# A decoder kernel's selective scan: the carried state is copied by GpSimd at its own wait instead of by VectorE, under new instruction orders

## The reference

```
x = layernorm(x + L0_attn(x))            # selective scan (below)
x = layernorm(x + L0_xattn(x, ctx))      # similarity, norm, softmax
x = layernorm(x + L0_ffn(x))             # 8 experts of width 176, top 2, and a shared one of 352
x = layernorm(x + L1_attn(x))            # gated linear recurrence
x = layernorm(x + L1_xattn(ctx, x))      # top-76 mask of a 256x256 similarity, per batch
x = layernorm(x + L1_ffn(x))             # 8 experts of width 128, top 2, and a shared one of 256
```

```
hidden = silu(conv(W_in x) + bias)            dts = softplus(W_dt dt + b_dt)
dA[n]  = exp(dts * A[:, n])                   dBu[n] = dts * B[n] * hidden
state[n] = dA[n] * state[n] + dBu[n]          (along the 256 positions)
y = sum over n of C[n] * state[n] + D * hidden
```

## Time and profile before

| | |
|---|---|
| median of 3 runs | 695.41 us |
| the profiled execution | 695.28 us, span 693.5 us |
| VectorE busy | 574.6 us (83% of the span) |
| TensorE busy | 553.7 us (80%) |
| ScalarE busy | 440.4 us (64%) |
| GpSimd busy | 228.8 us (33%) |
| mean granted TensorE clock | 0.873 |
| chain that ended last | PE 37%, DVE 35%, issue 14%, ACT 11% |

### The profile page before, as it was taken

The page is one execution under the profiler, slowest core; times in us unless marked ns, Lnnn a source line. Parts: engine busy times, 40 slices in busy tenths (PEclk is TensorE's granted clock), DMA queues, the critical chain, the costliest instruction groups (busy, mean ns, idle before and its releaser), DMA issues.

```text
span 693.5 us, 8972 instructions
## 1 busy us (share of the span) xinstructions
PE 553.7 (80%) x2504; PEld 395.2 (57%) x2504; DVE 574.6 (83%) x1307; ACT 440.4 (64%) x959; POOL 228.8 (33%) x280
## 2 busy tenths in 40 slices
PE   5753454988799875999899799888499999979957
PEld 3532242666567653667656575656366766657634
DVE  1179999999899979999999998999998999672442
ACT  3688354878689364889784879397167988232211
POOL 1055555423223345434332452343023435010000
PEclk9976575898799975899999989999589999989968
DMA  6580100570053400660162010461054037006000
GB/s 211 165 351 0 60 1 1 143 255 1 1 149 104 132 8 1 169 229 1 54 194 64 28 63 1 115 222 54 1 170 152 2 113 209 1 12 207 2 8 8
DMA packets 29297, 63.56 MB, mean 92 GB/s; under 512 B 4864, under 2 KB 8192, under 8 KB 28736
## 3 DMA queue, kind: packets, MB, share of 16 engines
q1 hardware_dynamic: 29248, 62.98, 29.4%
HBM read 61.85 MB, written 1.11 MB: 91 GB/s over the span
## 4 chain that ended last, share of the span: by engine, by line
PE 37%; DVE 35%; issue 14%; ACT 11%; DMA 1%; DVEq 1%; POOL 0%; SPq 0%; POOLq 0%; ACTq 0%
PE work L545 24%; DVE st L1077 8%; DVE acc L1093 6%; PE h_bank L521 4%; PE work L596 4%; ACT dA L877 3%; PE work L521 3%; DVE carry L1101 3%; DVE h_tok L1001 3%; DVE m L1042 2%; DVE wk L1046 2%; DVE row L937 2%; DVE bst L929 2%; ACT L877 1%; ACT xsT L757 1%
## 5 line engine op out<-in xcount | busy, mean ns | idle before, releaser
L496 POOL TENSOR_TENSOR dbu<-du,b_rows 128x512 f32<-128x512 f32 x128 | 165.2, 1292 | 139.5 <-DVE st L1077 112.7
L877 ACT ACTIVATE dA<-dts,a_neg 128x128 f32<-128x128 f32 x512 | 160.1, 390 | 31.2 <-DVE st L1077 30.6
L1077 DVE TENSOR_TENSOR_SCAN st<-dA,dbu 128x516 f32<-128x516 f32 x128 | 165.4, 1295 | 3.2 <-issue 2.0
L521 PE MATMUL h_bank<-ident,st 128*128 128x128 f32 x512 | 93.9, 315 | 59.3 <-DVE st L1077 59.0
L521 PEld LDWEIGHTS h_bank<-ident,st 128*128 128x128 f32 x512 | 70.3, 162 | 95.4 <-DVE st L1077 76.9
L545 PE MATMUL work<-stream,xsT 128*128 128x352 f32 x320 | 116.0, 504 | 0.5 <-ACT h_tok L757 0.3
L1093 DVE SCALAR_TENSOR_TENSOR acc<-h_bank,c_cols,acc 128x512 f32<-128x512 f32 x128 | 93.2, 728 | 12.2 <-PE h_bank L521 11.7
L545 PEld LDWEIGHTS work<-stream,xsT 128*128 128x128 f32 x320 | 63.0, 211 | 28.8 <-issue 7.9
L757 ACT ACT_TABLE_LOAD x46 | 59.0, 1283 | 7.4 <-PE work L545 6.7
L877 ACT ACT_TABLE_LOAD x46 | 59.0, 1283 | 0.8
L1001 DVE SCALAR_TENSOR_TENSOR h_tok<-h_tok,wf,work 128x128 f32<-128x128 f32 (+2 forms) x136 | 43.6, 372 | 18.9 <-PE work L545 18.7
(11 more groups left out here) (154 smaller groups left out, 860.7 us busy)
## 6 DMA issues: line engine op xcount, KB each, us to landing
stream<-in_stream SPq DMA_DIRECT2D x80, 352.0 KB, 3.6
stream<-in_stream SPq DMA_DIRECT2D x32, 384.0 KB, 3.8
b_rows<-b_dram SPq DMA_DIRECT2D x32, 256.0 KB, 5.4
stream<-in_stream SPq DMA_DIRECT2D x8, 256.0 KB, 3.3
wg<-in_wg SPq DMA_DIRECT2D x1, 1280.0 KB, 8.2
wu<-in_wu SPq DMA_DIRECT2D x1, 1280.0 KB, 10.8
wd<-in_wd SPq DMA_DIRECT2D x1, 1280.0 KB, 13.3
xT<-in_xT SPq DMA_DIRECT2D x4, 256.0 KB, 4.0
```

Of the source, the lines that this page charges most:

```text
L496: gp.tensor_tensor(tile[:, :, 1:1 + w * P], du[:, batch % 2, :, lo:hi], b_rows[:, b % 2, k:k + 1, :].to_broadcast([P, ET, P]), ALU.mult).t ...
L521: return nc.tensor.transpose(dst, src, ident[:, :])
L877: last = A(dA[:, i % DA_RING, t, 1:1 + w * P], dts[:, batch % 2, t, lo:hi], ACT.Exp, scale=a_neg[:, t, k:k + 1])
L1077: V.tensor_tensor_scan(st[:, i % ST_RING].rearrange("p t l -> p (t l)"), dA[:, i % DA_RING].rearrange("p t l -> p (t l)"), dbu[:, i % DBU_ ...
```

## The change

GpSimd's loop gets the copy: ahead of dbu number i, behind the wait for scan number i - 3 that it makes anyway, it copies the last column of that scan into `carry` (if that scan belongs to an even group). VectorE's copy and its two waits are taken out. The four strings of `ORDER` and `BANK` are replaced.

```diff
 ORDER = {
     "pe": [
-        "pp000apppssppaaaaaaaaaaaaaspssppsssssssssssssss0s00sss00000sssss0000s0s00s00s000s0000s000sss00000s000101s00spp",
+        "ppa0aaaaaaaaaaaaa00pppssppsspssppssssssssssssss0s00sss00000sssss0000ss000s00s000s000s0s00ss000000s000saaspps01",
...
     "dve": [
-        "saa00111pppppppppsssssssapsssssssssassa00sss0s00ss0s0s0s00as00s0s00s000sa000000ss0000000assaasa0aa00000sas0s00",
-        "pppp010saaaa1a0100a100a11p0s0000011s1s11s000000ss111s000000011111aasasa0a000aas1s11111ssa00sss0aaas00s0s0s0s00",
+        "saa00111ppppaaaaapppppsssssssasspsssssssaassa00assas0s00ss0s0s0s00s00s0s00s000s000s000s0000000ssass0aaas00000s",
+        "pppp0a00a1sss1s0101s11011p100s11s00ss011100000s11111ss000000ssaaas0000000aass0s000001s1111sa0a001aa0s0s0s00s00",
...
     "act": [
-        "p0p00appspaaaaaaaaaaapssspsssppssspssssssssssss000ssss00sss000ss0s0000s00s000000ss0000000ss0000sss000aaa1000s1",
+        "pa0paaaaaaaaaaa00ppsppssspssspspssspsssssssssss000ssaaass00sss000ss0s0000ss00000ss0000000000ss0000ssss000asp00",
...
@@ -486,6 +486,12 @@
                     if i >= DBU_RING:
                         pool.wait_ge(s["scan_done"], i - DBU_RING + 1)
+                    g, n = divmod(i - DBU_RING, N)
+                    if g >= 0 and hands_on(g):
+
+                        if hands.index(g):
+                            pool.wait_ge(s["carried"], (hands.index(g) - 1) * N + n + 1)
+                        gp.tensor_copy(carry[:, n, :], st[:, (i - DBU_RING) % ST_RING, :, P]).then_inc(s["carry_ready"], 1)
                     tile = dbu[:, i % DBU_RING]
@@ -1094,12 +1100,6 @@
                                 .then_inc(s["acc_done"], 1)
-                        if hands_on(b):
-                            dve.wait_ge(s["scan_done"], b * N + n + 1)
-                            if hands.index(b):
-                                dve.wait_ge(s["carried"], (hands.index(b) - 1) * N + n + 1)
-                            V.tensor_copy(carry[:, n, :], st[:, (b * N + n) % ST_RING, :, w * P])\
-                                .then_inc(s["carry_ready"], 1)
                 if stage == "out" and k == 2:
```

More of the change, by code:

```diff
@@ L88 @@
     "pe": [
-        "pp000apppssppaaaaaaaaaaaaaspssppsssssssssssssss0s00sss00000sssss0000s0s00s00s000s0000s000sss00000s000101s00spp",
[L90 to L94, removed]
+        "ppa0aaaaaaaaaaaaa00pppssppsspssppssssssssssssss0s00sss00000sssss0000ss000s00s000s000s0s00ss000000s000saaspps01",
+        "aaaaaaaaaaaaa00111pspp1111s0s0000ss1111101s000s00s01s1111100s00s010sss0000000s001s000s0011s101s00s11000001111s",
+        "ss0000s0s00s00s00s00s000sssa000000s00s000a11s1101s100s1spp011s100001s111s111aaaaaaaaaaaaa1s110000s0001111s000s",
+        "000s0000010s01s11ss11100s000s111s111001s1110s111s00pspp1111s0s0000ss1111s11s1s111s011sss111100000000s0s000000s",
+        "000s00s000s000ss101s00ss11s0000011110000s00000s00saa0sssaaaaaaaaaaaaa00010s0000001000001110100s110110000sa1111",
+        "11s11110s0000001111s000s00s000s0s000s00000000s1s1111s1s1s11110100111101000011111110000000100000000000000000111",
         "111111111111111111111111111111111111",
@@ L97 @@
     "dve": [
-        "saa00111pppppppppsssssssapsssssssssassa00sss0s00ss0s0s0s00as00s0s00s000sa000000ss0000000assaasa0aa00000sas0s00",
-        "pppp010saaaa1a0100a100a11p0s0000011s1s11s000000ss111s000000011111aasasa0a000aas1s11111ssa00sss0aaas00s0s0s0s00",
[L100 to L103, removed]
+        "saa00111ppppaaaaapppppsssssssasspsssssssaassa00assas0s00ss0s0s0s00s00s0s00s000s000s000s0000000ssass0aaas00000s",
+        "pppp0a00a1sss1s0101s11011p100s11s00ss011100000s11111ss000000ssaaas0000000aass0s000001s1111sa0a001aa0s0s0s00s00",
+        "s0s00s000ss000000s1a0000000ss1aaa1ss011s0000011s1ss01100111ss011111s0s0100s00111110s100000s1000s1000000000011s",
+        "s11ss1pppp11s111s0s0000011111ass1s1111s10s00s1s101s110s110100s11ss11111111spssaa0010111100ss000000aaas00000000",
+        "00ssss0s00000sss0s0010a01a0100aaa00s0a00s000s000saaa1ss00011saa0000000aaaa0a000a00aaa11s101100111as0a111110s01",
+        "00s11110010s00000ss000ss0001s000000011s011s00011sss111s1110011111000101111010100100101100000000000000000001101",
         "111111111111111111111111111111111111",
@@ L106 @@
     "act": [
-        "p0p00appspaaaaaaaaaaapssspsssppssspssssssssssss000ssss00sss000ss0s0000s00s000000ss0000000ss0000sss000aaa1000s1",
[L108 to L112, removed]
+        "pa0paaaaaaaaaaa00ppsppssspssspspssspsssssssssss000ssaaass00sss000ss0s0000ss00000ss0000000000ss0000ssss000asp00",
+        "01saaaaaaaaaaap111p1111ss00pssp000s111110s11000000s1s1111ss0000001111s0s000000ss0000ss000s1000ss1s11001111aaas",
+        "000ss0s0000s00sss000000000ss0000s0000sss0001as1111000s11ssp10011s11s1111s0001saaaaaaaaaaa1110s0000111100s000ss",
+        "000000000011111sss110000s0111s111111s00ss1s000p111ssp1111sp00ssps1000s1111ss11111011s1111ss0000s00000s0s00000s",
+        "0000ss0000ss000s1000ss1s11s0011110000aaa0ss000000000a00ss0aaaaaaaaaaa1000000ss0000s000000aaa111111s10011s11111",
+        "1000s11011s0000001111s000s0000s000000ss0000ss0001ss11111111111000111100111100011110000000100000000000000000111",
         "111111111111111111111111111111111111",
@@ L115 @@
     "pool": [
[L116 to L121, removed]
+        "ppppppppppppppppppppsaaaaaaaaaaaaaaaaaaaaaaaaaaaaaaaaaaaaaaaaaaaaaaaaaaaaaaaaaaaa0000ssssssssss1111sssssssssss",
+        "sss000sss00ss000000000000000000000000ssssssssssss000000ss000sss1s0011111111111111111s000000000000000000000000s",
+        "sssssssssss000000s111111ss00000ss000000000000000000000000ssssssssss111111111111111111ss000000ssss000ss00ss0000",
+        "00000000000000000000111111ss1sss1s1111111111111111ssss000000sss111111ss000ss1s1001111111111111111ss00000000000",
+        "0000000000000ssssss111111sssssss000000ssss000s0010000000000000000000000001ssssss1111111111111111s000000s000s00",
+        "s000000000000000000000000111111ssssss1s11111111111111111s000000ss000111111000000000000000000000000001111111111",
         "111111110011111111111111111111111111",
@@ L126 @@
 BANK = [
[L127 to L130, removed]
+    "01234502341502341502341502341502345012340512304152413502413505124305123405135024153245321453125341205341205120",
+    "51205201520314523015423054124512542541254124251245124125415413054310254310543210532410354210354203154230154201",
+    "35421305412305412305412305142031450324105231051420534120453104251304521452142531240351240532140531420531420531",
+    "24503124503124053124503125403125403124",
 ]
```

## The result

The changed kernel takes 677.67 us (median of 4 runs, 676.23 to 680.23) against 695.88 of the kernel before: a ratio of 0.9739 with a 95% interval of 0.9703 to 0.9776, 18 us or 2.6% faster. Measured once more with the last group of experiments it gave 676.54 us, ratio 0.9698 (0.9674 to 0.9723). Forecast were 681.3 us, in a range of 667 to 698. The profiled execution took 677.89 us, with a span of 676.1.

What follows compares the result with a forecast made beforehand. VectorE was taken to bound the scan stretch; +2.4 - 19.8 - 7.2 = -24.6 us on it, of which 0.57 reaches the end, gave 695.3 - 14.0 = 681.3 us, range 667 to 698.

Steps and rivals of the forecast that it cites:

- The bound: Scan stretch goes at VectorE's pace (94% busy, TensorE 81%); the last 100 us, led by TensorE, stay.
- What a copy is: VectorE's 64 copies, 791 ns each, are mostly a wait for GpSimd's product to end.
- Rival 1: All 64 copy steps of some 0.72 us leave, scans not inheriting the wait: 642 us; chance 0.05.
- Copies with a scan behind them: 24 places on VectorE where the scan inherits the wait: +0.1 us each, 2.4 us in all.
- Copies with another held operation behind them: 7 places on VectorE where another operation GpSimd holds up follows: nothing gained (ends 0 and 0.15 us each).
- the walk's 0.6 us for each free place: Copies with other work behind them on VectorE: 0.6 us less each at 33 places, 19.8 us.
- The idle start: Five rounds of batch 0's top-k mask move into VectorE's idle start: 7.2 us leave the full stretch.
- the share of VectorE's time that reaches the end: Of VectorE's 24.6 us, 0.57 reaches the end, as for copies with other work behind them: 14.0 us.
- Rival 2: Wait is handed on and almost nothing reaches the end: at most 3 us gained, 692 to 698 us; chance 0.12.
- Rival 3: GpSimd becomes late: copies delay products (9.6 us) and 16 meet scans (13.6 us): 704.5 us; chance 0.12.
- Rival 4: Only VectorE's idle start is won: 4.1 us, 691 us; inside the forecast range, no chance of its own.

Runs made afterwards that it cites:

- experiment 4: Kernel before, with VectorE's copy made as a one-element maximum reduction at the same place, old orders: 688.07 us, ratio 0.9885.
- experiment 5: Kernel before, with VectorE's copy made as a one-element maximum reduction and with the new orders and banks: 676.42 us, ratio 0.9706.
- experiment 12: Changed kernel with GpSimd's 128x512 product replaced by a fill with a constant: 655.38 us, ratio 0.9405 to the kernel before.
- experiment 3: Changed kernel with the first five rounds of batch 0's mask put back behind the seventh scan step: 683.91 us, ratio 0.9828 to the kernel before.
- experiment 10: Changed kernel's code under the orders of before, with only their start laid anew: 685.03 us, ratio 0.9815 to the kernel before.
- experiment 1: Changed kernel's code (GpSimd copies) with the orders and banks of before: 681.50 us, ratio 0.9783 to the kernel before.
- experiment 2: Code of the kernel before (VectorE copies) with the new orders and banks: 683.74 us, ratio 0.9816 to the kernel before.

## Why the prediction was right, point by point

**The bound.** VectorE's busy share of the scan stretch and the unchanged last 100 us: right. The last scan starts at 576.4 us, forecast 579, and 98.5 us follow its end.

**What a copy is.** Right, and shown: a wait for GpSimd's product that depends on the kind of the operation (experiments 4, 5 and 12). Rival 1, that all of the copies' time goes, and 642 us, are out: the scans' mean rose to 1.434 us, forecast 1.445.

**Copies with a scan behind them.** +0.1 us each was taken, 0.05 to 0.06 measured (2.51 or 2.52 to 2.57). Right in sign and near in size.

**Copies with another held operation behind them** were put at nothing, the wait moving onto them. It moved, and onto later norms too: 6.7 us more on L943, 20 of 48 held up instead of 9. That belongs to the walk's 0.6 us for each free place, and VectorE's sum bears it out: 24.6 us less were forecast, 22.8 measured.

**The idle start.** 7.2 us of rounds moved: they run from 20.3 to 27.5 us, the first scan is not later (41.2 us). Against one block among the first scans that is worth 6 to 7 us at the end (experiment 3), with 4.1 in the sum. Against the places that the old string gave the rounds it is worth nothing (experiment 10).

**The step that was mis-sized** is the share of VectorE's time that reaches the end: "With that share for all, 24.6 x 0.57 = 14.0." The span fell by 17.4 us with VectorE's busy time in the stretch 22.8 less, 0.76. The share was read off the chain for the copies alone, and the runs have no one share: 13.8 of 21.1 us reach the end of experiment 1's profiled execution, 0.65, and 21 of 46 in experiment 12, 0.46. As a term for the strings, too, it was low: the orders alone brought 13 us (experiment 2) where only the rounds' 4.1 were counted, and 4.1 was itself more than the rounds' move is worth under the old orders. That the total came within 4 or 5 us is thus partly luck: the code alone brought 15 us where its terms give 9.9 (17.4 x 0.57), the orders alone 13 instead of 4.1, and the 7 to 10 us by which these two overlap stood nowhere in the sum. The profiled execution of experiment 2 (686.9 us) is the longest of its five; in it the scan stretch is shorter by 7.1 us, just the rounds, so that how much of the 13 lies beyond them can't be read from it.

**Rival 2**, nothing reaches the end, is refuted by the code alone (0.9783). **Rival 3**, a late GpSimd, too: a second copy in its queue costs nothing that can be measured (0.9722), and the 0.13 us more ahead of each product is seen only in the dense period. Its copies do meet running scans, and the prediction took nothing for that: 5 of the 64 take 0.8 to 1.12 us, so that their mean is 252 and not 190 ns. The rival had 16. Even before, four of GpSimd's copies were held up in this way, 1.04 to 1.14 us each, and not one, as the prediction says. **Rival 4** named the idle start as the only gain: the code alone, without it, brings 15 us (experiment 1).

## What to carry to other kernels

An instruction whose usual duration is several times that of its shortest case may be a wait in disguise: look for what ends with it, here GpSimd's product, and ask what stands behind it before taking it away, since the next operation that GpSimd holds up inherits the wait. Moving the 4 values to GpSimd, to ScalarE, or leaving them on VectorE as an operation of another kind all gave the same time under the new orders; the cheapest cure was the kind of the operation. And gains of code and of order don't add: 15 and 13 us made 18 to 21.

## What the runs showed of the hardware that was not expected

The same chain of TensorE's instructions, with the same waits of 1.71 and 0.47 us ahead of it, ran at a granted clock of 1.00 (2.4 GHz) in the profiled execution of experiment 1 and at the lower level, 1.2 GHz, in that of experiment 10, where four matmuls of 128x352 took 2.69 instead of 1.43 us. Two such stretches cost 6.1 us between the two traces, and executions of experiment 10 itself lie 7 us apart.

A norm, whose one large input lies in SBUF, is held up by a GpSimd fill that only writes (0.54 against 0.41 us), a scan with two is not (1.22 us). Beside GpSimd's product, with over 0.3 us of it left, VectorE's copies, scans and norms have a mean of 0.86, 1.83 and 1.15 us instead of 0.18, 1.23 and 0.41 (the traces of the kernels before and after and of experiments 2 and 4 together); the mask's maximum (0.41), its replacement (0.41), the one-element reduction (0.15) and the products with PSUM (L1001, 0.39) take the same as without it.
